# A recommender tower on one core: the second relu of each layer goes to VectorE, which adds it to the first, and the step numbers of the pipeline are laid out anew

## The reference, cut to what matters

```python
for i in range(3):
    z = einsum('bfe,bge->bfge', x, xk).reshape(B, 256, 256)   # product of fields f and g
    z = einsum('bcl,oc->bol', swapaxes(z, 1, 2), Ws[i]) + bs[i][None, :, None]
    z = relu(z)                       # b x 16 x 256
    z = sum(z, axis=-1)               # b x 16
    outs.append(z)
    xk = broadcast(z[:, :, None], (B, 16, 256))
h = concatenate([concatenate(outs, 1), dense_ctx], 1)   # 2048 x 64
h = relu(h @ W_top1 + b_top1)                           # x 512
h = relu(h @ W_top2 + b_top2)                           # x 256
y = h @ W_top3
```

## Time and profile before

| what | value |
|---|---|
| median of 3 runs | 611.44 us (611.04 to 613.63) |
| profiled execution, time | 614.28 us |
| its span, first to last instruction | 612.5 us |
| mean granted TensorE clock | 0.989 |
| busy: PE, DVE, POOL, ACT | 566.3, 494.5, 463.1, 437.6 us |

### The profile page before, as it was taken

The page is one execution under the profiler, slowest core; times in us unless marked ns, Lnnn a source line. Parts: engine busy times, 40 slices in busy tenths (PEclk is TensorE's granted clock), DMA queues, the critical chain, the costliest instruction groups (busy, mean ns, idle before and its releaser), DMA issues.

```text
span 612.5 us, 18145 instructions
## 1 busy us (share of the span) xinstructions
PE 566.3 (92%) x7680; PEld 329.1 (54%) x7680; DVE 494.5 (81%) x220; ACT 437.6 (71%) x1234; POOL 463.1 (76%) x565
## 2 busy tenths in 40 slices
PE   1778889999999999999999999999999999999776
PEld 1334445555555565655556555555556565555444
DVE  5898899888888988888889888888899888887100
ACT  2466677768778776878878777887877786886542
POOL 5989888888878887888878888888878788862000
PEclk9999899999999999999999999999999999999978
DMA  4422222222222222222222122222222222210000
GB/s 98 115 76 73 62 62 71 61 62 63 61 62 63 61 63 63 61 63 61 63 63 65 58 64 62 60 63 61 63 64 63 68 61 59 59 45 1 1 1 2
DMA packets 14788, 35.89 MB, mean 59 GB/s; under 512 B 5921, under 2 KB 6305, under 8 KB 14689
## 3 DMA queue, kind: packets, MB, share of 16 engines
q0 software_dynamic: 12288, 33.57, 19.3%
q1 hardware_dynamic: 2418, 1.16, 0.8%
HBM read 34.70 MB, written 0.01 MB: 57 GB/s over the span
## 4 chain that ended last, share of the span: by engine, by line
PE 68%; DVE 20%; issue 7%; ACT 3%; POOL 2%; DMA 0%; SPq 0%; DVEq 0%; POOLq 0%; ACTq 0%
PE sum_ps L521 29%; DVE prods L222 19%; PE turn_ps L501 9%; PE outer_ps L564 9%; PE wide_ps L585 7%; PE sum_ps L541 5%; PE wide_ps L576 4%; PE outer_ps L559 3%; ACT relu_k L431 2%; POOL emb L262 2%; PE sum_ps L536 1%; PE wide_ps L593 1%; PE sum_ps L547 0%; PE sum_ps L533 0%; DMA id_lim<-id_limits 0%
## 5 line engine op out<-in xcount | busy, mean ns | idle before, releaser
L222 DVE TENSOR_TENSOR prods<-turn_ps,emb_t 128x3360 f32<-128x3360 f32 x128 | 462.2, 3646 | 11.8 <-ACT emb_t L404 8.9
L262 POOL DMA_INDIRECT emb<-tables,rows_sb x256 | 252.1, 985 | 44.9 <-issue 31.1
L521 PE MATMUL sum_ps<-prods,w_sb 128*32 128x272 f32 x4096 | 267.1, 400 | 2.5 <-POOL prods L222 2.3
L521 PEld LDWEIGHTS sum_ps<-prods,w_sb 128*32 128x32 f32 x4096 | 126.0, 110 | 94.0 <-issue 14.5
L421 ACT ACTIVATE relu<-sum_ps,bias_sb 128x120 f32<-128x120 f32 x256 | 91.8, 370 | 100.8 <-PE sum_ps L521 96.6
L272 POOL TENSOR_TENSOR prods<-emb_t 128x256 f32<-128x256 f32 x128 | 94.8, 741 | 53.8 <-ACT emb_t L404 50.3
L431 ACT ACTIVATE relu_k<-outer_ps 128x2048 f32<-128x2048 f32 x64 | 120.9, 1889 | 4.5 <-PE outer_ps L564 4.4
L501 PE MATMUL turn_ps<-ident_sb,emb 128*128 128x128 f32 x512 | 90.7, 295 | 29.7 <-DVE prods L222 10.9
L403 ACT COPY emb_t<-turn_ps 128x512 f32<-128x512 f32 x128 | 76.1, 595 | 44.2 <-PE turn_ps L501 36.2
L501 PEld LDWEIGHTS turn_ps<-ident_sb,emb 128*128 128x128 f32 x512 | 55.1, 143 | 88.8 <-issue 49.0
L411 ACT ACTIVATE prods<-emb_t 128x512 f32<-128x512 f32 x128 | 83.0, 649 | 0.1
(11 more groups left out here) (41 smaller groups left out, 269.2 us busy)
## 6 DMA issues: line engine op xcount, KB each, us to landing
emb<-tables,rows_sb POOLq DMA_INDIRECT x256
w_sb<-w_top SPq DMA_DIRECT2D x1, 512.0 KB
ids_sb<-ids_t SPq DMA_DIRECT2D x1, 128.0 KB, 2.0
h<-dense_t SPq DMA_DIRECT2D x1, 128.0 KB
w_sb<-w_top SPq DMA_DIRECT2D x1, 128.0 KB
ident_sb<-ident SPq DMA_DIRECT2D x1, 64.0 KB
w_sb<-w_cols SPq DMA_DIRECT2D x1, 64.0 KB
wp_sb<-w_proj SPq DMA_DIRECT2D x1, 32.0 KB
```

The costliest lines, as they stand in the source:

```text
L222: eng.tensor_tensor(out, every, shifted, ALU.mult).then_inc(done, 1)
L262: nc.gpsimd.indirect_dma_start(out=emb[:, k % EMB_RING, t * E:(t + 1) * E], out_offset=None, in_=tables, in_offset=bass.IndirectOffsetOnAx ...
L521: last = nc.tensor.matmul(sum_ps[s * 2 * F:(s + 1) * 2 * F, 0:SUM_COLS], w_sb[:, c, odd, :], x[:, c, 2 * s + odd, :, :], start=c == 0 and ...
```

## The change

The relu of each layer's second round leaves ACT. DVE takes it with one `scalar_tensor_tensor` (maximum with 0, then add) that adds the first round's relu in the same instruction, once for each layer and group, at the slots `RELU_ADD`. The sum over g then has half as many terms left, and `fold` has 8 matmuls in place of 16. GpSimd takes 3 of the 32 product blocks (336 elements) and DVE 29 (3248 elements). All slots but a few are given new numbers; `LAST_SLOT` becomes 152.

```diff
-POOL_BLOCKS = 2
+POOL_BLOCKS = 3
-PROJ, Z0_FIN, TURN_P, Z0_DIAG, Z0_SUM = 10, 9, 11, 9, 10
-Z_BUILD = (11, 15)
-ROUNDS = (12, 16)
-FOLD = (14, 19)
-REDUCE = (15, 20)
-Z_T, HIDDEN1, HIDDEN2, OUTPUT = 21, 23, (25, 28), 31
+PROJ, Z0_FIN, TURN_P, Z0_DIAG, Z0_SUM = 11, 9, 13, 9, 10
+Z_BUILD = (11, 16)
+ROUNDS = (12, 17)
+RELU_ADD = (15, 20)
+FOLD = (15, 20)
+REDUCE = (17, 22)
+Z_T, HIDDEN1, HIDDEN2, OUTPUT = 23, 24, (29, 30), 32
...
+            def relu_add(k, g):                                    # on DVE
+                n = ROUND_NO[k, g, 1]
+                dve.wait_ge(outer_done, n + 1)
+                dve.wait_ge(outer_relu, n)
+                at_least(dve, fold_done[k], g)
+                nc.vector.scalar_tensor_tensor(out=relu_k[:, k, 1, :], in0=outer_ps[:].rearrange("p j n -> p (j n)"), scalar=0.0,
+                                               in1=relu_k[:, k, 0, :], op0=ALU.max, op1=ALU.add).then_inc(outer_relu, 1)
...
             for slot in range(LAST_SLOT + 1):
                 products(slot)
+                for k in range(2):
+                    if (g := group_at(slot, RELU_ADD[k])) is not None:
+                        relu_add(k, g)
...
-                if slot - 1 in ROUND_AT:                           # on ACT
-                    relu_round(*ROUND_AT[slot - 1])
+                for k in range(2):
+                    if (g := group_at(slot - 1, ROUNDS[k])) is not None:
+                        relu_round(k, g)
...
                 pe.wait_ge(outer_relu, ROUND_NO[k, g, TURNS - 1] + 1)
-                for q in range(G4):
+                x = relu_k[:, k, 1, :].rearrange("p (j h n) -> p j h n", j=J, h=HALF_G)
+                for h in range(HALF_G):
                     for j in range(J):
-                        last = nc.tensor.matmul(wide_ps[j * R:(j + 1) * R, 0:F * F], fold_sb[:],
-                                                relu_k[:, k, q // HALF_G, j, q % HALF_G, :], start=q == 0, stop=q == G4 - 1)
+                        last = nc.tensor.matmul(wide_ps[j * R:(j + 1) * R, 0:F * F], fold_sb[:], x[:, j, h, :],
+                                                start=h == 0, stop=h == HALF_G - 1)
```

More of the change, by code:

```diff
@@ L109, in build @@
         proj_b = sb("proj_b", [P, PT_RING, F * 2 * F])
-        relu_k = sb("relu_k", [P, 2, TURNS, J, HALF_G, F * F])
+        relu_k = sb("relu_k", [P, 2, TURNS, J * HALF_G * F * F])
         ids_sb = sb("ids_sb", [P, TILES], INT32)
@@ L425, in relu_pairs, with relu_round @@
                                          bias=bias_sb[:, 0:1]).then_inc(relu0_ready, 1)
-            def relu_round(k, g, q):
-                act.wait_ge(outer_done, ROUND_NO[k, g, q] + 1)
+            def relu_round(k, g):
+                n = ROUND_NO[k, g, 0]
+                act.wait_ge(outer_done, n + 1)
                 at_least(act, fold_done[k], g)
-                nc.scalar.activation(relu_k[:, k, q, :, :, :].rearrange("p j h n -> p (j h n)"),
-                                     outer_ps[:].rearrange("p j n -> p (j n)"), ACT.Relu).then_inc(outer_relu, 1)
+                nc.scalar.activation(relu_k[:, k, 0, :], outer_ps[:].rearrange("p j n -> p (j n)"), ACT.Relu).then_inc(outer_relu, 1)
             def take_side(what, g):
```

## The result

The changed kernel takes **657.62 us** (median of 4 runs, 655.82 to 657.91) against 611.76 before: a ratio of 1.0738 (95% interval 1.0707 to 1.0770), slower by 7.4%. The forecast was 632 us with a range of 618 to 648. The sign was right and the place was right; of the +46 us that came, the forecast had +20.6, less than half. The profiled executions have spans of 655.4 and 612.5 us, so +42.9 us are to be found, where the prediction had +20.6.

What follows compares the result with a forecast made beforehand. PE was taken to set the 34.88 us period; afterwards a closed loop of 36.4 would. Full periods +20.0, first period -0.3, start +2.0, ends -1.1 gave +20.6 on 611.44: 632 us, range 618 to 648.

Steps and rivals of the forecast that it cites:

- The work that moves: Work per group on each engine after the change: PE 32.5 us, ACT 23.4, DVE 34.1, POOL 30.8.
- The start: First slots, paced by GpSimd: its third block adds 0.23 us in some nine slots, +2 us.
- The loop: Closed chain DVE, PE, ACT through one group, with PE waiting for transpose and reduce: 36.4 us against 34.88, +1.5 a group.
- step 2: PE after DVE's transpose: wake 0.05, last sum matmul 0.12, fold1 1.00, round to its relu 1.33 us.
- step 5: PE after DVE's reduce: 0.05, last sum matmul 0.12, hidden1 0.89, turn 0.59, sums 1.97, round to relu 1.33 us.
- step 6: ACT after the round of slot 17: 0.3 us late (bounds 0 and 0.6), then 2.67 for relu and copies.
- the first period: First group, with no fold1 or hidden1 of a group before, hence no such wait: 34.1 + about 0.5, -0.3 us.
- The end: Behind the last sums: halved folds give back some 4.5 us, relu_adds and late fold0, reduce, spread cost; together -1.1.
- A: Rival: both waits absorbed, DVE's work of 34.1 us sets the period, faster, about 601 us; chance 0.09.
- B: Rival: the loop exists but steps overlap 1.3 to 1.7 us a group more, no change, 608 to 614; chance 0.06.
- C: Rival: slower still, by a dearer relu_add (up to 670 us) or GpSimd third block (640 to 647); chance 0.12.

Runs made afterwards that it cites:

- the relaid kernel: Changed kernel with reads one slot behind their writes, fold1 and hidden1 moved apart, third z_cat buffer: ratio 1.0205 with four GpSimd blocks, 0.9944 with three.

## Why the prediction was wrong

**The work that moves: right.** DVE is busy 33.93 us of a period (34.1), POOL 30.54 (30.8), ACT 24.15 (23.4). A fold takes 0.98 us from its start to the next piece where it is not interrupted (1.00). Only PE's busy time is off, 34.37 against 32.5; it holds the modelled ends of matmuls at every stop, and in the relaid kernel it is 33.04. GpSimd's blocks cost nothing in the loop, as said.

**The start: right in sum.** +2.0 forecast for GpSimd's third block, +2.0 measured. With two blocks the first transpose comes at 64.59 in place of 65.84, although DVE's products are longer there, so at least 1.25 of it is the block's; the rest wasn't taken apart.

**The loop: the right loop, two steps too short.** The walk again, each step with what the period from 321.31 shows:

| step | predicted | measured |
|---|---|---|
| 1, relu_add, products(13), transpose | 6.37 | 6.35 |
| 2, PE to the start of the relu | 2.50 | **3.00** |
| 3, ACT to products(15) | 2.67 | 2.67 |
| 4, DVE to the end of the reduce | 13.51 | 13.50 |
| 5 and the 0.3 of 6, PE to the relu | 5.25 | **5.95** |
| 6, ACT to products(20) | 2.67 | 2.66 |
| 7, products(20) | 3.45 | 3.45 |
| sum | 36.42 | 37.58 |

The steps that failed are **2 and 5**, each by its term "last of 16 sum matmuls 1.97 / 16 = 0.12", and 5 also by the price of hidden1. The division by 16 takes the matmuls as one behind the other. In the trace their records start four at a time, within 0.02 us, and the next four 0.23 us later: the four parts of `sum_ps` are worked on side by side. The last matmul, alone behind its wait, has its two records at 327.72 and 327.97, and the bias follows 1.19 us behind the second. So step 2 took 0.06 + 0.25 + 1.19 = 1.50 to the bias instead of 1.17. In step 5 it was 347.46 - 346.83 = 0.63 to hidden1 instead of 0.17, and 1.09 for hidden1 instead of 0.89, which was the row of another matmul shape.

This is no cost of the wait. The run with the early transpose does the same fold without a wait in front (first three lines), and the relaid kernel its hidden1 (last three):

```profile
281.23 1.05 PE L600 MATMUL wide_ps<-relu_k,fold_sb 128*32 128x256 f32 x16
282.21 0.39 PE L573 MATMUL outer_ps<-bias_wide,ones_sb 32*128 32x512 bf16 x4
283.60 1.88 ACT L445 ACTIVATE relu_k<-outer_ps 128x2048 f32<-128x2048 f32 x1 [0.51 <-PE outer_ps L578]
...
311.58 2.04 PE L533 MATMUL sum_ps<-prods,w_sb 128*32 128x272 f32 x32
313.55 1.16 PE L606 MATMUL wide_ps<-h,w_sb 64*128 64x128 f32 x8
314.64 0.66 PE L513 MATMUL turn_ps<-ident_sb,emb 128*128 128x128 f32 x4
```

From the last sum matmul's first record to the bias it is 1.42 us there and 1.44 behind the wait, from its second record to hidden1 0.32 in both, and hidden1 takes 1.09 in both. Without a wait the last matmul's time is shared with the other three parts of `sum_ps`; behind the wait it lies in the loop alone.

That gives 0.33 in step 2 and 0.46 + 0.20 in step 5. The rest of step 2 is 0.17 from the bias to the relu (1.50 against 1.33), and it stays open: PE's records of the round are the same, and the distance is 1.34 behind the same kind of wait in the run with half a relu_add and 1.39 without a wait in the lines above. The 1.67 in step 5 is ACT's lateness, the 0.3 of step 6: its square starts at 352.26, and the relu follows at its end; 0.34 was measured. In all that is 1.20 us a group, and the other steps give 0.04 back.

13 periods at 1.16 make 15.1; the first period, taken at -0.3, was +1.3 (35.80 against 34.52), 1.6 more. The boundaries used above cut the loop at other places than the transposes do, which takes 1.9 off, and leaves the 14.9 us by which the loop was off (34.6 less 19.7).

That it was this loop is shown by what moved it: one read early (35.59, expected 35.7), half a relu_add (35.49, expected 35.5) and two blocks (38.1, expected 38.2) came out as the walk made for each had said; both reads early gave most of what was expected (35.1, expected 34.3). What the walk couldn't do is tell apart the shares of the two reads (12 us off), nor see what late reads cost a PE that is full (+1.00 where it had none), nor the waits for the round at the old slots.

**The end: wrong sign.** -1.1 forecast, +6.3 measured. The folds gave back what was taken: three of 1.93, 3.64 and 3.40 us became 1.07, 1.07 and 1.94, 4.9 us less (4.5 forecast). What the sum put at nothing is the clock of everything else: no term let the small matmul groups behind the last fold run at the lower level, and for the last 22 us they did. Filling the waits gave back 5.6 of the 6.3.

**The range.** It let step 6 vary by 0.3 and the ends by 2 us. The 0.12 was the lowest price that the last sum matmul could have, and no bound above stood beside it. Bounded by the full length of one such matmul (0.42), twice, and with hidden1 at 1.16, its own duration, the walk would have reached past 37.

**Rivals.** A, that DVE would run at its own 34.1, was wrong for this layout (DVE waits 3.6 us a period) and right for the relaid one. B fails: the steps overlap less than taken, not more. C named the right side, and its span of 640 to 670 holds the result, but by the wrong prices: relu_add and the block cost what was forecast.

**The rule on the most occupied engine.** The Trainium skill, Perfetto Trace Analysis, section Identifying the Most-Contended Engine, says to optimize the engine with the highest occupancy first. The prediction counted TensorE by its matmuls, 92%, and so had the change as a gain by that rule. TensorE was relieved by 256 matmuls (512 records), and the time rose by 7.4%. But the section doesn't take TensorE's matmul time; it names the share of its weight loads instead, and that was 54%. Read so, DVE with 81% was the engine to relieve, and the change gave it 53 us more. Neither reading has the loop: in the period PE was full, and the same work on DVE gave a loss of 7.4% and, with the layout changed as well, a gain of 0.6%. The engine with the most work is a bound only once no loop through several engines is longer.

## What to carry to other kernels

Before work is moved between engines in a kernel whose queues follow a fixed order, walk one period through all engines and close the loop: its length, not the largest busy share, is the time. Two read-out slots of one shared tile were worth 2.4 us a period here, half of two relu_adds 2.1. Don't price a piece that will stand alone by dividing a stretch in which several run side by side: take the start-to-start distance of the same piece, with the same shape and the same successor. When a new kernel sits at the same period whatever is changed in it, look for the one engine whose timeline has only issue gaps.

## What the hardware showed that I had not expected

**A small DVE instruction held by GpSimd.** `z_rows` (16 elements, both inputs in SBUF) takes 0.17 us alone. It took 1.54 in the relaid kernel with four blocks:

```profile
333.43 1.54 DVE L362 SCALAR_TENSOR_TENSOR z_rows<-pair_sum,own_sum 128x16 f32<-128x16 f32 x1
```

GpSimd there:

```profile
332.93 1.00 POOL L223 TENSOR_TENSOR prods<-emb_t 128x448 f32<-128x448 f32 x1
333.89 1.04 POOL L298 TENSOR_TENSOR z_wide<-z_cat,sample_sb 128x512 f32<-128x512 f32 x1
```

It ends at 334.97, 0.04 us behind the second of two GpSimd operations, and had let both pass. In the period of the changed kernel shown above GpSimd is idle when `z_rows` runs, and it lasts 0.17. The products and relu_add, which read one input from PSUM, were never held: in the changed kernel they last 3.50 to 3.54 and 2.28 to 2.29 us every time, whatever GpSimd does meanwhile. The Trainium skill, SBUF — State Buffer, section SBUF: two separate sides, says that a DVE instruction with two SBUF inputs and a GpSimd one that reads SBUF exclude each other: the one that starts first keeps the other out for the whole instruction. The traces agree in the hold; that DVE lets a second GpSimd operation go first is more than the section says. Removing the instruction from the relaid kernel with four blocks, where GpSimd set the period, gave nothing; no run here has the hold in a kernel that DVE bounds.

**TensorE's clock in a drain.** With waits of up to 2.5 us between short groups of matmuls the granted clock was 0.72 over 45 us, and a fold took 1.94 us instead of 1.07. Transposes of no use in those waits held it at 1.00 and shortened the end by 5.6 us; in the relaid kernel, at a mean of 0.989, they gave nothing.

**Matmuls that run side by side.** The 16 sum matmuls take 1.97 us to the next piece, four at a time in steps of 0.23, with 0.32 from the last step to a piece of another shape. One of them alone, in front of such a piece, takes 0.58 behind a wait and 0.55 in the stream, not 1.97 / 16 = 0.12.
